# A second tile of each ring round fetched row by row, from SyncE and ScalarE, with byte addresses in registers

## The reference

```python
h = relu(layernorm(x)) @ enc_w + enc_b
h_list = [h]
for l in range(3):
    e = edge_attr @ edge_w[l] + edge_b[l]
    msg = relu(h_list[l][src] + e)
    agg = segment_sum(msg, dst, num_segments=n_nodes)
    z = (1 + eps[l]) * h_list[l] + agg
    z = relu(z @ mlp_w1[l] + mlp_b1[l]) @ mlp_w2[l] + mlp_b2[l]
    h_list.append(relu(z))
out = x + concatenate(h_list, axis=1) @ out_w + out_b
```

## Time and profile before

| | |
|---|---|
| median of 3 runs | 6243.44 us (6243.08 to 6244.88) |
| the profiled execution | 6233.49 us, its span 6231.7 us |
| mean granted TensorE clock | 0.576 |
| GpSimd busy | 4667.1 us, 75% |
| TensorE busy | 4832.8 us, 78% |
| VectorE busy | 1645.1 us, 26% |
| ScalarE busy | 987.6 us, 16% |

### The profile page before, as it was taken

The page is one execution under the profiler, slowest core; times in us unless marked ns, Lnnn a source line. Parts: engine busy times, 40 slices in busy tenths (PEclk is TensorE's granted clock), DMA queues, the critical chain, the costliest instruction groups (busy, mean ns, idle before and its releaser), DMA issues.

```text
span 6231.7 us, 86632 instructions
## 1 busy us (share of the span) xinstructions
PE 4832.8 (78%) x14396; PEld 3004.4 (48%) x14397; DVE 1645.1 (26%) x4181; ACT 987.6 (16%) x1583; POOL 4667.1 (75%) x4998
## 2 busy tenths in 40 slices
PE   7887777777777777777777777777777777777777
PEld 5554444444444444444444444444444444444444
DVE  6322222222222222222222222222222222222222
ACT  4111111111111111111111111111111111111111
POOL 6777777777777677777777777767777777777776
PEclk8555555555555555555555555555555555555555
DMA  4222222222222222222222222222222222222223
GB/s 140 66 64 64 62 64 64 64 64 62 64 64 64 63 63 64 63 63 64 64 64 64 62 64 64 64 62 61 60 61 61 61 61 60 61 61 60 59 60 96
DMA packets 209009, 408.00 MB, mean 65 GB/s; under 512 B 93779, under 2 KB 106684, under 8 KB 207948
## 3 DMA queue, kind: packets, MB, share of 16 engines
q0 software_dynamic: 156960, 321.77, 19.8%
q10 hardware_dynamic: 22096, 59.87, 3.3%
q1 hardware_dynamic: 29508, 22.58, 1.1%
HBM read 378.16 MB, written 25.69 MB: 65 GB/s over the span
## 4 chain that ended last, share of the span: by engine, by line
POOL 40%; PE 22%; issue 15%; DMA 14%; DVE 5%; ACT 4%; DVEq 0%; POOLq 0%; ACTq 0%
POOL rows L383 40%; DMA rows<-h_table,idx 14%; PE bank L634 14%; PE bank L630 6%; DVE rows L887 4%; ACT rows L551 4%; PE bank L653 0%; PE bank L655 0%; PE bank L608 0%; PE bank L600 0%; DVE onehot L751 0%; DMA out_acc<-x_t 0%; PE bank L593 0%; DVEq L957 0%; PE bank L661 0%
## 5 line engine op out<-in xcount | busy, mean ns | idle before, releaser
L383 POOL DMA_INDIRECT rows<-h_table,idx x4905 | 4630.1, 944 | 1525.8 <-issue 1266.7
L634 PEld LDWEIGHTS bank<-onehot,rows 128*128 128x128 f32 x9966 | 2087.3, 306 | 2784.9 <-ACT rows L551 2659.0
L634 PE MATMUL bank<-onehot,rows 128*128 128x64 f32 x9966 | 2235.3, 400 | 1347.8 <-ACT rows L551 1347.0
L630 PE MATMUL bank<-edgew,attr 65*128 65x512 f32 x2496 | 2235.2, 1008 | 9.3 <-DMA w2s<-w 9.3
L887 DVE TENSOR_TENSOR rows<-bank,rows 128x512 f32<-128x512 f32 x1248 | 861.0, 690 | 4037.0 <-DMA rows<-h_table,idx 3913.5
L551 ACT ACTIVATE rows<-rows 128x512 f32<-128x512 f32 x1248 | 784.3, 628 | 5156.6 <-DVE rows L887 5156.6
L630 PEld LDWEIGHTS bank<-edgew,attr 65*128 65x128 f32 x2496 | 665.0, 310 | 270.2 <-issue 270.2
L873 DVE TENSOR_TENSOR onehot<-bank,dst_rel 128x256 f32<-128x256 f32 x1248 | 518.1, 415 | 204.7 <-issue 204.7
L883 DVE TENSOR_TENSOR agg_t<-bank,agg_t 128x64 f32 x1248 | 269.6, 216 | 288.6 <-PE bank L634 288.4
L653 PE MATMUL bank<-agg_t,w1s 128*128 (+1 forms) x150 | 149.2, 1098 | 1.5 <-DVE agg_t L883 1.5
L674 PE MATMUL bank<-outw,h_t 128*128 128x128 f32 x588 | 148.8, 396 | 0.7 <-ACT h_t L514 0.7
(11 more groups left out here) (82 smaller groups left out, 459.6 us busy)
## 6 DMA issues: line engine op xcount, KB each, us to landing
rows<-h_table SPq DMA_DIRECT2D x9984, 0.5 KB
rows<-h_table,idx POOLq DMA_INDIRECT x4905, 2.5
attr<-ea_t ACTq DMA_DIRECT2D x155, 256.0 KB, 3.6
h_table<-h_n ACTq DMA_DIRECT2D x48, 256.0 KB, 2.1
h_table<-rows SPq DMA_DIRECT2D x24, 256.0 KB, 2.7
out<-out_acc SPq DMA_DIRECT2D x24, 256.0 KB, 3.1
out_acc<-x_t ACTq DMA_DIRECT2D x4, 1280.0 KB, 16.7
rows<-dst_g SPq DMA_DIRECT2D x1, 832.0 KB
```

The source lines that it names most:

```text
L383: return g.indirect_dma_start(dst, None, h_table[l % 2], bass.IndirectOffsetOnAxis(ap=index, axis=0))
L630: return nc.tensor.matmul(dst[0:EP, 0:tiles * D], cols, edgew[:, l, 0:tiles * D], start=True, stop=True)
L634: last = nc.tensor.matmul(dst[:, 0:WIN], rows[0:EP, slot, j, :], onehot[0:EP, hot_slot, j, :], start=(j == 0), stop=(j == tiles - 1))
```

## The change

Line numbers are those of the kernel before.

- `SHARED_GROUP` (slot 13) loses its tile 3 to row transfers as `SYNC_GROUP` (slot 14) has. GpSimd issues three gathers for each of the two.
- Of slot 13's 128 rows SyncE issues 48, ahead of the 128 of slot 14. ScalarE issues the other 80: eight after the relu of each of groups 0 to 9 of a round, in `fetch_rows`, with a register load of eight ahead of them. After the relu of group 0 ScalarE also waits for `agg_done` of slot 13.
- VectorE multiplies all node numbers by 512 once, at the end of `find_units`, so `row_at` holds byte addresses. The table is seen as bytes (`h_bytes`), and the loaded register is handed over (`donate=True`) and not copied. SyncE loads 16 registers at a time.
- VectorE waits at groups 13 and 14 for 128 row transfers each.
- The 24 stores of `out` in the last layer go from SyncE to ScalarE, after the relu of group 5 of the half, where the other layers have `store`.

```diff
-FK, FJ = 14, 3
-LOADS = 32
+SYNC_GROUP, SHARED_GROUP = 14, 13
+SHARED_BY_SYNC = 48
+CHUNK = 16
+ACT_ROWS = 8
...
+    h_bytes = [h.rearrange("n d -> (n d)").bitcast(u8) for h in h_table]
...
-        row_idx = sb("row_idx", [1, (NFULL + 1) * EP], i32)
+        row_at = sb("row_at", [2, (NFULL + 1) * EP], i32)
...
+        def table_row(l, eng, at):
+            byte = eng.snap(at, donate=True, min_val=0, max_val=(NR * P - 1) * (D * 4))
+            return h_bytes[l % 2][bass.ds(byte, D * 4)].rearrange("(a d) -> a d", a=1)
...
-                    sp.dma_start(row_idx[0:1, :].rearrange("a (b e) -> a b e", e=EP),
-                                 src_g.rearrange("(b t) e -> b t e", t=RING * TG)[:, FK * TG + FJ, :]
-                                 .unsqueeze(0)).then_inc(row_idx_in, 16)
+                    for u, k in enumerate((SYNC_GROUP, SHARED_GROUP)):
+                        of_group = src_g.rearrange("(b t) e -> b t e", t=RING * TG)[:, k * TG + TG - 1, :]
+                        sp.dma_start(row_at[u:u + 1, :].rearrange("a (b e) -> a b e", e=EP), of_group.unsqueeze(0))\
+                          .then_inc(row_at_in, 16)
...
-                def fetch_tile(b):
-                    for first in range(0, EP, LOADS):
-                        sp.load(row, row_idx[0:1, bass.ds(b * EP + first, LOADS)])
-                        for i in range(LOADS):
-                            at = sp.snap(row[i], min_val=0, max_val=NR * P - 1)
-                            sp.dma_start(rows[first + i:first + i + 1, FK, FJ, :], table[bass.ds(at, 1), :])\
-                              .then_inc(fetched, 16)
+                def fetch_rows(b, u, group, count, fetched):
+                    for first in range(0, count, CHUNK):
+                        with ExitStack() as held:
+                            at = [held.enter_context(sp.register(f"sync_at{next(named)}")) for _ in range(CHUNK)]
+                            sp.load(at, row_at[u:u + 1, bass.ds(b * EP + first, CHUNK)])
+                            for i in range(CHUNK):
+                                row = rows[first + i:first + i + 1, group, TG - 1, :]
+                                sp.dma_start(row.bitcast(u8), table_row(l, sp, at[i])).then_inc(fetched, 16)
+
+                def fetch_body(b):
+                    def freed(group):
+                        before = l * NG + group + 1 + S0 - RING
+                        if not isinstance(b, int):
+                            wait_apart(sp, agg_done, b * RING + before)
+                        elif b or l:
+                            sp.wait_ge(agg_done, b * RING + before)
+
+                    freed(SHARED_GROUP)
+                    fetch_rows(b, 1, SHARED_GROUP, SHARED_BY_SYNC, shared_fetched)
+                    freed(SYNC_GROUP)
+                    fetch_rows(b, 0, SYNC_GROUP, EP, sync_fetched)
...
-                    sp.wait_ge(row_idx_in, 16)
                     sp.wait_ge(s_ready, 1)
                 else:
                     sp.wait_ge(stored, l * NU * 16 + 16)
-                    sp.wait_ge(agg_done, l * NG + FK + 1 + S0 - RING)
-                fetch_tile(0)
+                fetch_body(0)
                 with sp.Fori(1, NFULL) as b:
-                    wait_apart(sp, agg_done, b * RING + (l * NG + FK + 1 + S0 - RING))
-                    fetch_tile(b)
-                sp.wait_ge(agg_done, NFULL * RING + l * NG + FK + 1 + S0 - RING)
-                fetch_tile(NFULL)
+                    fetch_body(b)
+                fetch_body(NFULL)
                 far_passes(sp, load_extra(sp), far_pass)
-            with sp.Fori(0, ND) as i:
-                sp.wait_ge(o_added, i + ((L - 1) * NU + 1 + N0))
-                sp.dma_start(out[:, bass.ds(i * (UT * D), UT * D)].rearrange("p (t d) -> p t d", d=D),
-                             out_acc[:, bass.ds(i * UT, UT), :]).then_inc(s_out, 16)
...
-                    tiles = min(TG, NTR - group * TG) - (slot == FK)
-                    if slot != FK and tiles < TG:
+                    tiles = min(TG, NTR - group * TG)
+                    if slot in (SYNC_GROUP, SHARED_GROUP):
+                        tiles = TG - 1
+                    elif tiles < TG:
...
+            for u in range(4):
+                act.wait_ge(p_stored[u], (NI + 3 - u) // 4 * 16)
...
+                def store_out(i):
+                    act.wait_ge(o_added, i + (l * NU + 1 + N0))
+                    act.dma_start(out[:, bass.ds(i * (UT * D), UT * D)].rearrange("p (t d) -> p t d", d=D),
+                                  out_acc[:, bass.ds(i * UT, UT), :]).then_inc(s_out, 16)
...
-                    if l < L - 1:
-                        store(i)
+                    (store if l < L - 1 else store_out)(i)
...
+                def fetch_rows(b, first):
+                    with ExitStack() as held:
+                        at = [held.enter_context(act.register(f"act_at{next(named)}")) for _ in range(ACT_ROWS)]
+                        act.load(at, row_at[1:2, bass.ds(b * EP + first, ACT_ROWS)])
+                        for i in range(ACT_ROWS):
+                            row = rows[first + i:first + i + 1, SHARED_GROUP, TG - 1, :]
+                            act.dma_start(row.bitcast(u8), table_row(l, act, at[i])).then_inc(shared_fetched, 16)
...
-                        if kk in (2, 3, 5)[:3 if l < L - 1 else 2] and groups - half * HB >= HB:
+                        if kk in (2, 3, 5) and groups - half * HB >= HB:
                             with act.If(unit > 0):
-                                (relu_z if kk == 2 else relu_h if kk == 3 else store)(unit_before(unit))
-
+                                (relu_z if kk == 2 else relu_h if kk == 3 else
+                                 store if l < L - 1 else store_out)(unit_before(unit))
+                        if k == 0 and not (isinstance(b, int) and b == 0 and l == 0):
+                            wait_apart(act, agg_done, b * RING + (l * NG + SHARED_GROUP + 1 + S0 - RING))
+                        if k < (EP - SHARED_BY_SYNC) // ACT_ROWS:
+                            fetch_rows(b, SHARED_BY_SYNC + k * ACT_ROWS)
+
+                act.wait_ge(stored, l * NU * 16 + 16)
...
+                dve.wait_ge(row_at_in, 32)
+                own(v.tensor_scalar(row_at[:, :], row_at[:, :], float(D * 4), None, ALU.mult))
...
+                        by_rows = {SYNC_GROUP: sync_fetched, SHARED_GROUP: shared_fetched}
+                        if k in by_rows:
                             wait_apart(dve, e_done, first_group + (k + 1 + S0))
-                            take(dve, fetched, 16 * EP)
+                            take(dve, by_rows[k], 16 * EP)
                         else:
                             dve.wait_ge(e_done, first_group + (k + 1 + S0))
-                        dve.wait_ge(gathered[k], (b + (l * uses_of_slot(k) + 1)) * (16 * (TG - (k == FK))))
+                        dve.wait_ge(gathered[k], (b + (l * uses_of_slot(k) + 1)) * (16 * (TG - (k in by_rows))))
```

More of the change, by code:

```diff
@@ L3 @@
 from contextlib import ExitStack
+import itertools
 P = 128
@@ L28, in gnn_kernel @@
                eps, out_w, out_b, out, edges, nodes):
-    f32, i32 = mybir.dt.float32, mybir.dt.int32
+    f32, i32, u8 = mybir.dt.float32, mybir.dt.int32, mybir.dt.uint8
     ALU, ACT, AX = mybir.AluOpType, mybir.ActivationFunctionType, mybir.AxisListType
@@ L54, in gnn_kernel @@
     assert ND * UT + LAST == -(-nodes // P) and NB == -(-NG // HB) and NGP <= P * GR and NI <= NBU
-    assert REST == RING and FK < RING - 1 and EP % LOADS == 0
+    assert REST == RING and EP % CHUNK == 0 and SHARED_BY_SYNC % CHUNK == 0
+    assert (EP - SHARED_BY_SYNC) % ACT_ROWS == 0 and (EP - SHARED_BY_SYNC) // ACT_ROWS < SHARED_GROUP < SYNC_GROUP < RING - 1
     h_table = [nc.dram_tensor(f"h_table{u}", (NR * P, D), f32).ap() for u in range(2)]
@@ L194, in gnn_kernel @@
         gathered = sems("gathered", RING)
-        row_idx_in = sem("row_idx_in")
-        fetched = sem("fetched")
+        row_at_in = sem("row_at_in")
+        sync_fetched = sem("sync_fetched")
+        shared_fetched = sem("shared_fetched")
         e_done = sem("e_done")
@@ L307, in _ @@
                     sp.dma_start(outb[:, :], out_b.partition_broadcast(P)).then_inc(s_par, 16)
-            row = [sp.alloc_register(f"row{i}") for i in range(LOADS)]
+            named = itertools.count()
             for l in range(L):
-                table = h_table[l % 2]
                 def far_pass():
@@ L951, in edge_body @@
                             accumulate(k - 2)
-                        if k == FK:
+                        by_rows = {SYNC_GROUP: sync_fetched, SHARED_GROUP: shared_fetched}
+                        if k in by_rows:
                             wait_apart(dve, e_done, first_group + (k + 1 + S0))
-                            take(dve, fetched, 16 * EP)
+                            take(dve, by_rows[k], 16 * EP)
                         else:
```

(2 more changed lines are left out.)

## The result

The kernel with the change takes 6150.82 us (median of four runs, 6140.5 to 6154.15), the kernel before 6244.16 beside it (four runs, 6243.08 to 6246.46): a ratio of 0.9847, interval 0.983 to 0.9864 (estimated over all runs; the two medians alone give 0.985). That is 1.5% less; forecast was 6146 us, 1.56% less, in a range of 6132 to 6205. The profiled execution took 6140.5 us, its span 6138.7, against 6233.5 and 6231.7: 93.0 us less by the trace, where the sum of the prediction said 97.1.

The account below looks back on a forecast made before the run. GpSimd's gather queue was taken as the bound, SyncE barely hidden behind it. Gathers -97.4, end -1.7 and layer 0 +2 gave -97.1 on 6233.5, so 6136.4; with 9.95 for the median, 6146 us, range 6132 to 6205.

Parts of the forecast that it names:

- What bounds, and the gain: GpSimd's gather queue never rests in the loop; 78 gathers fewer at 1.2484 us each take off 97.4 us.
- The sum: Whole run: -97.4 for gathers, -1.7 at the end, +2 for layer 0, together -97.1 us on the profiled 6233.5.
- SyncE's row: SyncE's row fetch: without register arithmetic and one gap, a row falls from 0.4146 to 0.332 us.
- The load of 16: SyncE's register load of 16, absent from the earlier trace, put at 1.09 us between 0.93 and 1.25.
- the round: SyncE's work a round: 58.4 rows, 12.0 loads, 5.7 rest, 76.1 us, under GpSimd's 77.40 by 1.3.
- rival 3: SyncE's row addresses are still computed, giving a round of 90.7 us and a time of 7170 us; chance 0.03.
- the price of lateness: SyncE's round: each us over 77.40 costs about 75 us, plus 30 for layer 0's late start.
- The room of the ring: Behind a late slot 14 or late relus, some 60 us of lateness pass before GpSimd stops.
- Layer 0: SyncE's first load at 102.9 us, after up to 4.5 us of multiplication; 2 us allowed for the layer's late end.
- ScalarE's part at zero: ScalarE's load and eight rows after a relu take 3.8 us, under a group's 4.99, so cost zero.
- The end: Last layer's tail: moving the 24 stores of `out` off SyncE saves 1.7 us after the last gather.
- Rival 5: All 256 rows of a round meet on one DMA engine: about 3 us, or throttled gathers, chance 0.02.

Follow-up runs that it names:

- one_tile: Changed kernel with slot 13's tile gathered by GpSimd again, byte addresses, loads of 16 and moved stores kept: 6233.45 us, 1.0001 of the kernel before.
- sync32: Changed kernel with SyncE issuing 32 of slot 13's rows instead of 48 and ScalarE 96: 6138.08 us, 0.9848 of the kernel before.
- act_none: Changed kernel with ScalarE's 80 rows of slot 13 left out: 6137.88 us, 0.9847 of the kernel before.
- again: The changed kernel itself, measured once more: 6139.46 us, 0.985 of the kernel before.
- computed: Changed kernel with node numbers in the registers, copied and multiplied for each row, instead of byte addresses: 7310.12 us, 1.1699 of the kernel before.
- chunk8: Changed kernel with SyncE loading 8 registers at a time instead of 16: 6388.11 us, 1.0217 of the kernel before.
- sync64: Changed kernel with SyncE issuing 64 of slot 13's rows instead of 48 and ScalarE 64: 6512.09 us, 1.0445 of the kernel before.
- the third tile: Changed kernel with tile 3 of slot 12 also fetched as rows by ScalarE in every second round: 6883.69 us, 1.1041 of the kernel before.
- third_free2: Changed kernel plus slot 12's tile by ScalarE every second round, SyncE's 48 rows of slot 13 left out, on another chip: 6536.56 us, 1.047.
- half_gather: Changed kernel with the last gather of slot 12 bringing 64 rows instead of 128, one execution: 6136.69 us.
- after: The first profiled execution of the changed kernel: 6140.5 us, against 6233.5 for the kernel before.
- third_free: Changed kernel plus slot 12's tile by ScalarE every second round, SyncE's 48 rows of slot 13 left out: 8800.59 us beside 9750.99.

## Why the prediction was right

**What bounds, and the gain.** Right. 78 gathers fewer at 1.2484 are 97.4 us; the first to the last gather of a layer took 2042.25, 2039.85 and 2039.69 us before and take 2012.01, 2008.05 and 2007.86, in sum 93.9 less. one_tile shows that nothing else in the change gives any of it that the times can tell, sync32 and act_none that SyncE's margin and ScalarE's rows take no more than a few us.

**How close the number came is partly luck.** The sum, -97.1 us on the profiled execution, was 4 us too good. The 9.95 us that the prediction added for the median's distance to one execution fit the distance of the two levels of the gathers that the trace of `again` shows and that it did not know of. The first four times had their median 10.3 us above the profiled one again, and so 6150.82 stands beside 6146; in `again` the median is 6139.46, beside 6136.4 without that term. The range covers both. Against the kernel before, the gain is 92 to 93 us at either level.

**SyncE's row: 0.332 forecast, 0.318 at the median, 0.330 at the mean.** The argument from the code (arithmetic and one gap gone) held. The load of 16 was put at 1.09 and took 1.143; the round at 76.1 and took 75.3; the wait left at 1.3 and is 2.07. The wait of 12.4 that the prediction took from the earlier trace rows is a mean that has layer 0's shorter waits in it; 12.9 is that of layers 1 and 2, and with it the work before is 65.8 and not 66.3. computed and chunk8 each undo one term of this sum and both put SyncE over the gathers, at 92.3 (forecast for rival 3: 90.7) and 80.1 us. sync64 confirms the price of lateness that the rivals used, 75 us for each us and about 30 for layer 0: 343 + 30.

**The room of the ring.** Right as it was used, for sums that come late in a steady flow: with sync64 VectorE trails by 70 us before GpSimd is held. It was wrong to read it as room for anything that makes ScalarE late, as I did again in expecting 6,095 of the third tile. The prediction argued that all that stands behind a late relu has some 60 us; slot 13 stands behind it too, and since the change SyncE has only 2 us there. TensorE and VectorE, too, can follow a late ScalarE only at their own pace (see third_free2).

**Layer 0.** The allowance of 2 us was not needed. The multiplication of `row_at` took 1.88 us and not up to 4.5, and SyncE's first load comes at 99.6 us instead of 102.9. I took the tile of slot 14 in round 25 as 4 us late; in fact VectorE's addition for it, which in round 1 comes 41.5 us after the last gather of its group starts, gains about 2.2 us in every round, since SyncE's 75.2 is under the beat by 2.2 and not by 1.3, and from round 20 on it comes 2.6 us after, as in other groups. Five of VectorE's long waits for these rows, in the timeline of its additions, from early to late in layer 0:

```profile
260.04 0.69 DVE L928 TENSOR_TENSOR rows<-bank,rows 128x512 f32<-128x512 f32 x1 [15.98 <-DMA rows<-h_table]
...
1088.45 0.69 DVE L928 TENSOR_TENSOR rows<-bank,rows 128x512 f32<-128x512 f32 x1 [13.30 <-DMA rows<-h_table]
1163.57 0.69 DVE L928 TENSOR_TENSOR rows<-bank,rows 128x512 f32<-128x512 f32 x1 [13.21 <-DMA rows<-h_table]
...
1389.53 0.69 DVE L928 TENSOR_TENSOR rows<-bank,rows 128x512 f32<-128x512 f32 x1 [8.99 <-DMA rows<-h_table]
...
1539.94 0.69 DVE L928 TENSOR_TENSOR rows<-bank,rows 128x512 f32<-128x512 f32 x1 [4.56 <-DMA rows<-h_table]
```

**ScalarE's part at zero.** Right within a few us, by act_none. The load of eight took 0.723 where 0.60 was taken from VectorE, the row 0.317 at the median (0.358 at the mean) where 0.385 was, the group 3.5 us where 3.8 was. The Trainium skill ("DMA: Bandwidth & Descriptors", section "Issuing engines are not separate DMA queues") says that issuing DMAs from several engines saves only the sequencer's time to start them, which is usually small beside the DMA. That time is all that the change moves to ScalarE, and it is not small in this kernel, where sync64 and computed are 4% and 17% slower than the kernel before by the queue's time alone. Whether other engines could bring bandwidth no run here shows.

**The end.** The last addition came 5.30 us after the last gather began and comes 6127.76 - 6124.14 = 3.62 now, 1.7 less, as forecast:

```profile
6124.14 0.94 POOL L399 DMA_INDIRECT rows<-h_table,idx  x1 [0.30 <-issue]
...
6127.32 2.40 PE L673 MATMUL bank<-onehot,rows 128*128 128x64 f32 x10 [2.30 <-ACT rows L584]
...
6127.76 0.29 DVE L928 TENSOR_TENSOR rows<-bank,rows 128x128 f32<-128x128 f32 x1 [0.90 <-DMA rows<-h_table,idx]
...
6134.82 1.22 PE L713 MATMUL bank<-outw,h_t 128*128 128x128 f32 x4 [0.67 <-ACT h_t L535]
...
6136.54 0.40 SPq L363 DMA_DIRECT2D out<-out_acc  x1
```

But from there to the end it is 10.9 us instead of 9.9. Of this, 0.6 us come ahead of the last node unit: the sums of the last two groups now come so close that TensorE does ten matmuls in a row, and the step after has to wait for them. The other 0.5 are the unit's last four matmuls, which took 1.22 us where they took 0.74 before; why is open. Of 1.7 us 0.6 is left. The same matmuls before:

```profile
6228.31 0.74 PE L674 MATMUL bank<-outw,h_t 128*128 128x128 f32 x4 [0.67 <-ACT h_t L514]
```

**Where 4 us of the sum stayed.** The interval of the gathers grew by 0.4 ns, 4,824 times, 1.8 us; the two layer changes grew from 13.07 and 14.59 to 13.84 and 15.64, 1.8 us; the first wait of GpSimd in layer 0 and six short ones near VectorE's lags there, 1.7 us; the tail gave 0.6 and the start 0.3. So -97.4 + 1.8 + 1.8 + 1.7 - 0.6 - 0.3 = -93.0. At the second layer change the next layer's first gather comes 15.64 us after the last one:

```profile
4100.65 0.94 POOL L399 DMA_INDIRECT rows<-h_table,idx  x1 [0.30 <-issue]
4116.29 0.94 POOL L399 DMA_INDIRECT rows<-h_table,idx  x1 [14.69 <-issue]
```

The code has GpSimd wait for the table's last store, as before. In the trace that store has landed 14.46 us after the last gather's start, where it was 14.33; but the first gather then starts 1.18 us after the landing, where it started 0.26 us after it, at both layer changes. So 0.92 us of each are lost on GpSimd behind the landing. They are also there in again, sync32 and act_none, and not in one_tile (13.59 and 14.99 us in all) or half_gather, both with 0.26; half_gather issues all 256 rows, so the rows are not the cause, which stays open. **Rival 5**, one DMA engine for all rows, did not cost anything that shows: landings are at 2.5 us as before. SyncE's queue has 3,770 packets of 512 bytes more for 3,744 rows more, so a row is one packet, on one engine; which one no run here shows.

## What to carry over

When one queue never rests and each of its instructions has a fixed price, look for a whole instruction that another queue can do in its idle time, and count that queue's time per instruction in the trace, gaps and register loads included: here 0.1 us of arithmetic and gaps a row decided between 1.5% faster and 17% slower. Before a queue with 2 us of room in a round is filled, write down what it waits for each round, since all room upstream of that wait is spent with it. Cheaper work off the bound gives nothing by itself (one_tile), only what it makes room for.

## What the runs showed of the hardware

- **The indirect gather costs nearly the same for half the rows:** 0.944 us for 128 rows, 0.903 for 64 (half_gather), with 0.305 to the next one.
- **The same program has two levels of time, 12 us apart,** 6138 and 6150. In traces it is the gather: 944 ns, 1.2488 us from one to the next in after, 947 and 1.2513 in again, and 947 in sync32 and act_none, whose profiled executions were at the upper level too. The kernel before took 6232 to 6233 beside again, one_tile and chunk8, and 6243 to 6244 beside the first times and third_free2, each time within 5 us; its one trace is of the lower level (944 ns). Why there are two levels is open. The kernels' difference is the same at either; a comparison of medians that mixes them can be off by 0.2%.
- **Register loads from memory on SyncE** took 1.14 us for 16, 0.69 for 8, 2.04 for 32 and 0.52 for one: many registers in one load pay. (0.245 us plus 0.056 a register gives the first three, and not the one.)
- **A row transfer with its address in a register is issued every 0.318 us** on SyncE and 0.317 on ScalarE (medians); with a copy and two multiplications first it was 0.4146 and, in computed, 0.416.
- **On the chip of third_free** the kernel before took 9,751 us and not some 6,240; why is open.
